# A linear-attention transformer layer on eight cores: feed-forward over pairs of token blocks, normalizations moved to VectorE

## The reference

```python
def layernorm(x): return (x - mean(x)) / sqrt(var(x) + 1e-5)
# x: (8, 4096, 1024) fp32, 16 heads of 64
q, k, v = split(layernorm(x) @ w_qkv.T);  q = relu(q);  k = relu(k)
z   = 1 / (k.sum(tokens) . q + eps)             # one per head and token
ctx = v^T k                                     # one 64x64 matrix per head
attn = (ctx @ q) * z
x   = x + attn @ w_proj.T + b_proj
x   = x + relu(layernorm(x) @ w1 + b1) @ w2 + b2   # hidden width 4096
```

## Time and profile before

| | us |
|---|---|
| median of the 3 runs shown | 2077.53 (1998.59 to 2240.05) |
| the profiled execution | 1994.2 |
| span of its cores, first to last instruction | 1983.5 to 1992.8 |
| TensorE busy, of the 1992.8 of the slowest core | 1616.7 |
| DMA moved | 220.22 MB, 111 GB/s on the mean |

### The profile page before, as it was taken

One profiled execution on the slowest core, in us unless ns is written; L12 is line 12 of the kernel. 1 busy time (PEld: TensorE's weight loads), 2 busy tenths in 40 slices (PEclk: granted clock), 3 DMA queues, 4 the chain that ended last, 5 costly groups with the idle time before them and its releaser, 6 DMA issues.

```text
span 1992.8 us, 31844 instructions; the slowest of 8 cores (1983.5 to 1992.8 us)
## 1 busy us (share of the span) xinstructions
PE 1616.7 (81%) x12000; PEld 1122.5 (56%) x12000; DVE 553.6 (28%) x1183; ACT 438.6 (22%) x905; POOL 176.9 (9%) x282
## 2 busy tenths in 40 slices
PE   0000799999996698989989999899898998989968
PEld 0000243444443376866768667676686776867757
DVE  0001533333321424133241332323313234133210
ACT  0000232233232131231311303223032131231311
POOL 1000000000000012020120201202102021020110
PEclk9999899999998698988989889898898998998989
DMA  9999222111001415336143362432623416335143
GB/s 151 162 125 110 43 43 43 35 40 40 19 27 36 134 40 184 107 117 209 65 172 122 102 222 73 150 132 91 222 99 124 158 70 218 106 117 191 43 148 128
DMA packets 90003, 220.22 MB, mean 111 GB/s; under 512 B 4592, under 2 KB 70128, under 8 KB 72192
## 3 DMA queue, kind: packets, MB, share of 16 engines
q1 hardware_dynamic: 78000, 184.59, 26.8%
q0 software_dynamic: 11856, 33.59, 12.1%
HBM read 226.58 MB, written 33.55 MB: 131 GB/s over the span
## 4 chain that ended last, share of the span: by engine, by line
PE 56%; DVE 5%; issue 3%; POOL 3%; DMA 1%; DVEq 0%; ACT 0%; POOLq 0%; SPq 0%; ACTq 0%
PE PB L666 23%; PE PB L691 23%; PE PB L604 4%; POOL tmp L615 3%; DVE ln L621 2%; PE PB L535 1%; PE PB L548 1%; PE PB L537 1%; PE PB L454 1%; PE PB L509 1%; DMA qb<-qsc 1%; PE PB L514 0%; DVE qz L562 0%; DVE msq L412 0%; DVE rloB L432 0%
## 5 line engine op out<-in xcount | busy, mean ns | idle before, releaser
L666 PE MATMUL PB<-ln,w_sb 128*128 128x256 bf16 x4096 | 457.1, 274 | 34.2 <-DVE ln L621 33.6
L691 PE MATMUL PB<-hT,w2t 128*128 128x256 bf16 x4096 | 449.9, 273 | 3.6 <-ACT hT L676 2.1
L666 PEld LDWEIGHTS PB<-ln,w_sb 128*128 128x128 bf16 x4096 | 369.5, 97 | 122.1 <-issue 39.9
L691 PEld LDWEIGHTS PB<-hT,w2t 128*128 128x128 bf16 x4096 | 399.4, 98 | 54.0 <-issue 7.9
L676 ACT ACTIVATE hT<-PB,b1c_sb 128x256 bf16<-128x256 f32 x512 | 242.8, 474 | 448.6 <-PE PB L666 448.1
L332 PE MATMUL PAkv<-wqkv_sb,lnx 128*128 128x512 bf16 x1024 | 225.1, 382 | 0.0
L615 POOL TENSOR_TENSOR tmp<-x,rbcB 128x256 f32<-128x256 f32 x128 | 92.6, 724 | 1073.8 <-DVE rbcB L582 994.8
L699 DVE SCALAR_TENSOR_TENSOR outb<-PB,b2c_sb,x 128x256 f32<-128x256 f32 x128 | 61.9, 484 | 409.1 <-PE PB L691 409.1
L234 PE MATMUL PAst<-xa,ones 128*1 128x512 bf16 x64 | 18.3, 438 | 191.9 <-DMA xa<-xT 191.9
L332 PEld LDWEIGHTS PAkv<-wqkv_sb,lnx 128*128 128x128 bf16 x1024 | 100.2, 98 | 127.2 <-issue 9.6
L604 PE MATMUL PB<-attnT,wproj_sb 128*128 128x256 bf16 x1024 | 155.7, 321 | 10.1 <-DVE x L631 9.1
(11 more groups left out here) (91 smaller groups left out, 894.3 us busy)
## 6 DMA issues: line engine op xcount, KB each, us to landing
w2t<-w2bf SPq DMA_DIRECT2D x128, 1024.0 KB, 5.9
xb<-xT SPq DMA_DIRECT2D x16, 1024.0 KB, 10.3
outT<-outb SPq DMA_DIRECT2D x16, 1024.0 KB, 5.3
w_sb<-w POOLq DMA_DIRECT2D x1, 8192.0 KB, 92.8
w2bf<-w2r POOLq DMA_DIRECT2D x8, 1024.0 KB, 144.5
xa<-xT POOLq DMA_DIRECT2D x8, 1024.0 KB, 9.8
qsc<-qout SPq DMA_DIRECT2D x64, 128.0 KB, 1.8
qb<-qsc SPq DMA_DIRECT2D x16, 512.0 KB, 11.2
```

The source lines that it names most:

```text
L666: f1_mm = nc.tensor.matmul(PB[w % 2][:, 0:NB], w1_sb[:, c, w * 128:(w + 1) * 128], ln2[:, c, :], start=(c == 0), stop=(c == CK - 1))
L691: f2_mm = nc.tensor.matmul(PB[2 + d % 2][:, 0:NB], w2t[:, d % NW2BUF, w, :], hT[:, w, :], start=(w == 0), stop=(w == WK - 1))
```

## The change

1. FF1 and FF2 run once for two blocks, in the even turns from 2 to 16, over 512 columns. `ln2` and `hT` are twice as wide. Odd turns have no feed-forward part; there `emit_zden(b+1)` and `emit_zchain(b+1)` stand behind `emit_squaresB(b)`, and `emit_statsB(b)` follows.
2. w2 is therefore read 8 times instead of 16. Its loads move from SP's queue to GpSimd's: groups 0 to 2 are issued in the odd turn, 3 to 7 in the even one, all ahead of that turn's casts in GpSimd's order, each behind its wait for a free buffer.
3. Attention: the matmul with `ctxt` takes `qb` itself; DVE copies z's bank to SBUF (`zbcs`) and then multiplies the attention bank by it, straight into `attnT`. ACT has no part in it any more. `emit_negm2` is emitted after the sixth of these eight rounds, before after the eighth product of `qz`.
4. Second layer norm: both steps on DVE, the factor read from PB[4]; `rbcB` and its copy are gone, `tmp2` is a single buffer.
5. `x1` gets a third buffer, and the residual is loaded into `x1` itself (updated in place) instead of `xb`. Its load for block b+1 is issued at the end of turn b, behind that turn's output DMAs.
6. FF2's result is finished by two DVE operations of 256 columns for each group and stored by 8 DMAs of 256 KB from a double buffer.

```diff
-            xb = SBB("xb", [128, 2, CK, NB_B], F32)
-            x1 = SBB("x1", [128, 2, CK, NB_B], F32)
-            ln2 = SBB("ln2", [128, CK, NB_B], BF16)
-            hT = SBB("hT", [128, WK, NB_B], BF16)
-            outb = SBB("outb", [128, CK, NB_B], F32)
+            x1 = SBB("x1", [128, 3, CK, NB_B], F32)
+            zbcs = SBB("zbcs", [128, 2, NB_B], F32)
+            ln2 = SBB("ln2", [128, CK, 2 * NB_B], BF16)
+            hT = SBB("hT", [128, WK, 2 * NB_B], BF16)
+            outb = SBB("outb", [128, 2, 2 * NB_B], F32)
...
                 if b >= 1:
-                    bb = b - 1
-                    for d in range(CK):
-                        WG(nc.sync, s_mmf2, 8 * bb + d - NW2BUF + 1)
-                        s_w2[kw % NW2BUF].inc(nc.sync.dma_start(
+                    if b % 2 == 1:
+                        qld, dlist = (b - 1) // 2, range(0, NW2BUF)
+                    else:
+                        qld, dlist = b // 2 - 1, range(NW2BUF, CK)
+                    for d in dlist:
+                        WG(nc.gpsimd, s_mmf2, 8 * qld + d - NW2BUF + 1)
+                        kw = 8 * qld + d
+                        s_w2[kw % NW2BUF].inc(nc.gpsimd.dma_start(
...
+                    def emit_attn(p):
+                        if p == 0:
+                            WG(nc.tensor, s_qb[b % 2], 16 * (b // 2 + 1))
+                        elif p == 1:
+                            WG(nc.tensor, s_hev, 32 * ((b - 1) // 2))
+                        else:
+                            WG(nc.tensor, s_aev, 8 * b + p - 1)
+                        s_mmattn.inc(nc.tensor.matmul(PB[p % 2][:, 0:NB], ctxt[:, p, :],
+                                                      qb[:, b % 2, p, :], start=True, stop=True))
...
+                    for p in range(CK):
+                        emit_zbc(p)
+                        emit_attn(p)
+                    for p in range(CK):
+                        WG(nc.vector, s_mmzbc, 8 * b + p + 1)
+                        s_qz.inc(nc.vector.tensor_copy(zbcs[:, p % 2, :], PB[2 + p % 2][:, 0:NB]))
+                        WG(nc.vector, s_mmattn, 8 * b + p + 1)
+                        WG(nc.vector, s_qz, 8 * b + p + 1)
+                        s_aev.inc(nc.vector.tensor_tensor(
+                            attnT[:, p, :], PB[p % 2][:, 0:NB], zbcs[:, p % 2, :], ALU.mult))
+                        if p == 5 and b >= 1:
+                            emit_negm2(b - 1)
...
-                    s_pa2.inc(nc.gpsimd.tensor_tensor(
-                        tmp2[:, k % 2, :], x1[:, bb % 2, k, :], rbcB[:, :], ALU.mult))
+                    else:
+                        WG(nc.vector, s_lnx2, 8 * bb + k)
+                    s_pa2.inc(nc.vector.tensor_tensor(
+                        tmp2[:, :], x1[:, bb % 3, k, :], PB[4][:, 0:NB], ALU.mult))
                     WG(nc.vector, s_pa2, 8 * bb + k + 1)
                     s_lnx2.inc(nc.vector.tensor_tensor(
-                        ln2[:, k, :], tmp2[:, k % 2, :], PB[5][:, 0:NB], ALU.add))
+                        ln2[:, k, (bb % 2) * NB:(bb % 2 + 1) * NB],
+                        tmp2[:, :], PB[5][:, 0:NB], ALU.add))
...
-                if b >= 1:
-                    bb = b - 1
+                if b >= 1 and b % 2 == 1:
+                    if b + 1 < NBB:
+                        emit_zden(b + 1)
+                        emit_zchain(b + 1)
+                elif b >= 2:
+                    q = b // 2 - 1
+                    j0, j1 = 2 * q, 2 * q + 1
                     for w in range(WK):
...
-                            f1_mm = nc.tensor.matmul(PB[w % 2][:, 0:NB],
+                            f1_mm = nc.tensor.matmul(PB[w % 2][:, 0:2 * NB],
...
-                            f2_mm = nc.tensor.matmul(PB[2 + d % 2][:, 0:NB],
-                                                     w2t[:, d % NW2BUF, w, :],
+                            f2_mm = nc.tensor.matmul(PB[2 + d % 2][:, 0:2 * NB],
+                                                     w2t[:, kw % NW2BUF, w, :],
...
+                        for jj, blk in ((0, j0), (1, j1)):
+                            s_oev.inc(nc.vector.scalar_tensor_tensor(
+                                outb[:, d % 2, jj * NB:(jj + 1) * NB],
+                                PB[2 + d % 2][:, jj * NB:(jj + 1) * NB], b2c[:, d:d + 1],
+                                x1[:, blk % 3, d, :], ALU.add, ALU.add))
+                        WG(nc.sync, s_oev, 16 * q + 2 * d + 2)
+                        s_ost[d % 2].inc(nc.sync.dma_start(
+                            outT_r[:, d, j0 * NB:(j0 + 2) * NB], outb[:, d % 2, :]), 16)
+                if b >= 1 and b + 1 < NBB:
+                    t = b + 1
+                    if t >= 3:
+                        j = t - 3
+                        WG(nc.sync, s_lnx2, 8 * (t - 2))
+                        WG(nc.sync, s_sq2p, 8 * (t - 2))
+                        WG(nc.sync, s_cast2, 8 * (t - 2))
+                        WG(nc.sync, s_oev, 16 * (j // 2) + (16 if j % 2 else 15))
+                    s_xb[t % 3].inc(nc.sync.dma_start(
+                        x1[:, t % 3, :, :], xT_r[:, :, t * NB:(t + 1) * NB]), 16)
                 if b < NBB:
                     emit_statsB(b)
```

More of the change, by code:

```diff
@@ L129, in build_nc @@
             SA = lambda name, shape, dt: sta.enter_context(nc.sbuf_tensor(name, shape, dt))
+            ones1f = SA("ones1f", [1, 128], F32)
+            s_ones.inc(nc.vector.memset(ones1f[:, :], 1.0))
             wqkv_sb = SA("wqkv_sb", [128, CK, 3 * C], BF16)
@@ L481, in build_nc @@
                 if b >= 1:
-                    bb = b - 1
-                    for d in range(CK):
-                        if bb == 0 and d == 0:
-                            WG(nc.sync, s_w2pc, 16 * CK)
-                        WG(nc.sync, s_mmf2, 8 * bb + d - NW2BUF + 1)
-                        kw = 8 * bb + d
-                        s_w2[kw % NW2BUF].inc(nc.sync.dma_start(
-                            w2t[:, d % NW2BUF, :, :],
+                    if b % 2 == 1:
[3 more added lines that the diff above has]
+                    for d in dlist:
+                        if qld == 0 and d == 0:
+                            WG(nc.gpsimd, s_w2pc, 16 * CK)
+                        WG(nc.gpsimd, s_mmf2, 8 * qld + d - NW2BUF + 1)
+                        kw = 8 * qld + d
+                        s_w2[kw % NW2BUF].inc(nc.gpsimd.dma_start(
+                            w2t[:, kw % NW2BUF, :, :],
                             w2bf.ap()[d * 128:(d + 1) * 128, :, :]), 16)
@@ L538, in emit_zbc @@
                                                      zlo[:, :], start=False, stop=True))
-                    def emit_attn(p):
-                        WG(nc.tensor, s_qz, 8 * b + p + 1)
+                    for p in range(CK):
+                        emit_zbc(p)
+                        emit_attn(p)
+                    for p in range(CK):
                         if p == 0:
[L543 to L564, removed]
+                            WG(nc.vector, s_aev, 8 * b)
+                        WG(nc.vector, s_mmzbc, 8 * b + p + 1)
+                        s_qz.inc(nc.vector.tensor_copy(zbcs[:, p % 2, :], PB[2 + p % 2][:, 0:NB]))
+                        WG(nc.vector, s_mmattn, 8 * b + p + 1)
+                        WG(nc.vector, s_qz, 8 * b + p + 1)
+                        if p == 0:
+                            WG(nc.vector, s_mmproj, 8 * b)
+                        s_aev.inc(nc.vector.tensor_tensor(
+                            attnT[:, p, :], PB[p % 2][:, 0:NB], zbcs[:, p % 2, :], ALU.mult))
+                        if p == 5 and b >= 1:
                             emit_negm2(b - 1)
@@ L580, in build_nc @@
                                                  start=False, stop=True))
[L581 to L589, removed]
                 if b < NBB:
```

87 lines of the change are left out of this document (34 added, 53 removed).

## The result

| | before | after |
|---|---|---|
| median | 1998.76 us (1996.65 to 2001.53, 6 runs) | 2021.37 us (2019.77 to 2023.06, 8 runs) |
| ratio after to before | | 1.0112, 95% interval 1.0100 to 1.0124 |
| span of the slowest core, profiled | 1992.8 us | 2025.6 us |
| a pair of turns, mean on that core | 163.8 us | 167.5 us |
| mean granted TensorE clock, by core, profiled | 0.929 to 0.936 | 0.912 to 0.919 |

The changed kernel is 1.1% slower, and the interval leaves no doubt about the sign. The forecast was 2018 us.

What follows compares the result with a forecast made beforehand. TensorE was taken as the bound: two feed-forward loops at its rate, plus a serial stretch each turn. Pairs rising from 163.6 to 167.2 us and a changed last turn gave span 2016.7 against 1992.8, hence 2018 us; 8-in-10 range 1990 to 2052.

Steps and rivals of the forecast that it cites:

- The pair: An odd and an even turn together: 167.2 us predicted against 163.6 before, +3.6 us.
- the slow start of FF1: FF1 beginning at TensorE's lower clock: 0.5 us taken, paid once a pair instead of twice; bounds 0.5 to 1.9.
- The span: Whole profiled execution: 2016.7 us predicted against 1992.8 before, +23.9 us.
- Wide matmuls: FF1 and FF2 over 512 columns: 55.3 us each per pair, saving 1.4 us against the narrow rate.
- Attention on DVE: Attention's eight rounds, each a DVE copy then a dependent multiplication: 0.85 us a round, projection starting at M + 11.2.
- Net zero: From a turn's mark M to the projection's start: M + 11.2 both before and after the attention change.
- The odd tail: Odd turn's end, from last residual's start through squares and z's chain, with no feed-forward work covering it: 7.9 us.
- Rival 3: GpSimd's w2 loads late in FF2, near 30 us by the skill's factor; landing at 20 us gives 2098 us; chance 0.06.
- The residual's load: Odd block's load lands at most 13 us after FF2's end, first use at 14.9: hidden by 1.9 us.
- a whole turn: Time that even blocks' residual loads were said to have for landing.
- rival 1: Odd block's residual late beside GpSimd's w2 loads: 2.5 us late gives 2035 us, slower by over 2%; chance 0.12.
- within 2%: Outcome class for the whole kernel's time, neither under 1954 nor over 2034 us: chance 0.74.

Runs made afterwards that it cites:

- e2_narrow: Changed kernel with every feed-forward matmul of 512 columns issued as two of 256: 2033.09 us, ratio 1.0155 to the kernel before.
- e3_dve_only: Kernel before with only the changed attention and second layer norm, both on DVE; no pairs, narrow matmuls: 2002.19 us, ratio 1.0009 to the kernel before.
- e7: Changed kernel with the odd turns' casts on ScalarE instead of GpSimd: 2009.42 us, ratio 1.0048 to the kernel before.
- e1: Changed kernel with each pair's FF2 moved to the following odd turn, buffers rearranged to make room: 1985.96 us, ratio 0.9927 to the kernel before.

## Why the prediction was right, and where it was not

- *Mechanism and sum.* The pair was put at 167.2 us and took 167.5 on the slowest core; odd turn 30.4 against 30.61, even turn 136.8 against 136.84. In the even turn luck is in the number: mark to FF1 took 0.35 us more than reckoned and FF1 0.1, and the slow start of FF1, put at 0.5, did not appear, since all of FF1's runs before the last turn took 55.41 us. The last turn's 132.77 against 132.7 is of the same kind: FF1 started 0.2 us late and took 57.74 instead of 57.2, and the end behind FF2 took 3.1 instead of 4.0.
- *The whole.* The span was put at 2016.7 and was 2025.6. Of those 8.9 us, 7.1 are there before turn 0's first z matmul (665.64 against 658.51 us), in a part that the change doesn't touch; over the eight cores turn 1's mark lies at 675.2 to 684.2 us before and at 677.0 to 690.5 after, and why is open. The forecast took as its base one execution of 1994.2 us, 4.6 below the median before. The step, +23.9 us, stands beside +22.6 between the medians, so that 2021.37 is 3.4 us above the forecast.
- *Wide matmuls*, 215.9 ns each from a row of stage A: 55.3 us a run predicted, 55.41 measured, and e2_narrow prices the form at 11.7 us for the kernel (10.5 expected).
- *Attention on DVE* at 0.85 us a round: 0.86, projection at M + 11.3 (11.2). "Net zero" was read from one turn of the kernel before, one of its late ones. Over 15 turns that kernel's projection starts at M + 10.7 on the mean, the changed kernel's at M + 11.4. The pair of 163.6 us, a mean, already held those earlier starts. e3_dve_only puts the price of all the moved DVE work at 2.9 us, with an interval (0.9988 to 1.0030) that takes in both nothing and 6 us.
- *The odd tail*, 7.9 us: 7.82. e7 shortens it by 1.4 us and the kernel follows one for one. e1 puts it under FF2 and gains 5.1 us a pair, not 7.8, since it uncovers z's chain in the even turn.
- *w2*: after turn 1, in which nothing waits for them, the loads land in at most 7.9 us (11.2 in turn 1), under the cover of 13.8. Rival 3 did not happen. The prediction's 30 us, a load's whole time multiplied by the ratio of two figures for another transfer, has nothing behind it: no load came near.
- *The residual's load* was the term that was mis-sized. I took its longest landing before, 11.9 us, as the bound, and an issue 1.1 us behind FF2's end, and so 1.9 us of slack. The odd blocks' loads, the ones with that little slack, were issued 1.7 us behind it and landed in 9.4 to 14.2 us, 12.7 on the median; the latest landed 15.9 us after FF2's end, where 14.9 was the first use. What the prediction left out is the next block's load: "a whole turn" is its time to land, but SP issues it 2.3 us behind the odd one, and the two are in flight together.

```profile
1192.59 0.53 POOL L484 DMA_DIRECT2D w2t<-w2bf  x1 [6.38 <-PE PB L681]
...
1193.77 0.39 SPq L704 DMA_DIRECT2D x<-xT  x1
...
1196.11 4.79 SPq L704 DMA_DIRECT2D x<-xT  x1
```

  In that turn the first x load landed at 1206.50, the second at 1211.37, and the w2 load ahead of them at 1199.80. Of the two w2 loads that rival 1 named, the one of 6.9 us earlier had landed at 1191.72, before the residual was issued. Which of its neighbours held up the residual was not tried. The price is small: on the slowest core the first residual is 0.8 and 1.1 us late in turns 3 and 5 and in no other, and on most cores in none. One wait row of the changed kernel (waiter, what it waited for, us in all, times, longest):

```profile
DVE x L616 <- DMA x<-xT: 4.8, 2, 2.5
```

- *The reading of the sum* is the step that failed. The sum said +1.2%, 24 us, and the parts of it held. The prediction then gave 0.74 to "within 2%", on the ground that 2%, 40 us, "is about what a measurement of this kernel can tell from no change". No row is named for that figure. The runs showed a far finer measure: the changed kernel's eight executions lie within 3.3 us, the kernel before's six within 4.9, and the ratio is 1.0112 with an interval of 1.0100 to 1.0124. The forecast should have read "slower, by some 24 us". For the same reason it had to be set against the profiled execution alone: beside the median shown then, 2077.53 us, the figure 2018 looks like a gain of 2.9%, and it never was one.

## What to carry to other kernels

Before batching two iterations to halve the instruction count or the traffic, ask which of the two was the bound: here neither was (wide matmuls are worth 0.6%; half the w2 traffic should be worth nothing by the rows, since FF2 already ran unbroken, but that was not tried by itself), and the batch left every second turn's dependent chain with nothing beside it, which cost more. A serial stretch is paid by what TensorE could do in it, so count how many such stretches there are and what stands beside each end; delaying one ready piece of matmul work by a turn and cutting it into the gaps made the stretch longer and the kernel 8% faster. A small loss that a sum of rows shows can be measured: state it with its sign.

## What the runs showed of the hardware beyond that

- Eight DVE squares of 128x256 with both inputs in SBUF and eight GpSimd casts take 2.8 us each apart and 4.2 and 4.4 us together, less than one after the other.
- An operation on ScalarE that reads PSUM took 0.09 us longer with a bias operand at both widths: relu with bias 0.47 us against 0.38 for a copy over 256 columns (kernel before, L676 and L589), 0.69 against 0.60 for relu or copy without one over 512 (changed kernel, L666 against L285 and L347). It hid under 1.73 us of matmuls.
- Whether a load on GpSimd's queue is held up beside a wide DVE copy from SBUF to SBUF, the case that the prediction took up, was not tried: no such copy runs beside the w2 loads in any of these kernels.
